# Layer 1 of a recommendation tower: all four full steps as split products, the half step earlier, and one block of ten passes

## The reference

```
x0 = prev = stack of 32 gathered rows                   # [B, 32, D]
for W in (filter_0, filter_1):
    z    = einsum('bhd,bmd->bhmd', x0, prev)            # all pairs of fields
    prev = relu(einsum('bpd,pn->bnd', z as [b, h*m, d], W[0]))   # [B, 128, D]
    outs.append(prev)
z = sum over d of concat(outs)                          # [B, 256]
h = relu([z, dense_ctx] @ W_top1 + b_top1); h = relu(h @ W_top2 + b_top2)
y = h @ W_top3                                          # [B, 1]
```

## Time and profile before

| what | value |
|---|---|
| median of 3 runs | 951.88 us (946.05 to 952.69) |
| the profiled execution's own time | 947.22 us, span 945.3 us |
| TensorE busy | 881.0 us (93%) |
| GpSimd busy | 773.2 us (82%) |
| VectorE busy | 765.0 us (81%) |
| ScalarE busy | 691.3 us (73%) |
| granted TensorE clock | 0.998 of full speed |
| DMA | 58.13 MB, mean 61 GB/s |

### The profile page before, as it was taken

The page is one execution under the profiler, slowest core; times in us unless marked ns, Lnnn a source line. Parts: engine busy times, 40 slices in busy tenths (PEclk is TensorE's granted clock), DMA queues, the critical chain, the costliest instruction groups (busy, mean ns, idle before and its releaser), DMA issues.

```text
span 945.3 us, 17955 instructions
## 1 busy us (share of the span) xinstructions
PE 881.0 (93%) x3551; PEld 650.2 (69%) x3551; DVE 765.0 (81%) x2391; ACT 691.3 (73%) x2347; POOL 773.2 (82%) x582
## 2 busy tenths in 40 slices
PE   0289999999999999999999999999999999999989
PEld 0157777777777777777777777777777777777753
DVE  4068888889888888898888889988888899888893
ACT  2058777787878777878787778787877777877762
POOL 7768899888888999988889989887777877777772
PEclk9999999999999999999999999999999999999999
DMA  6031222222112222221122222211222222102000
GB/s 175 13 105 51 75 75 75 73 72 71 32 50 70 73 74 73 74 71 34 46 69 74 73 74 74 74 38 37 67 71 71 71 71 71 47 29 66 1 1 0
DMA packets 41436, 58.13 MB, mean 61 GB/s; under 512 B 7265, under 2 KB 16033, under 8 KB 41410
## 3 DMA queue, kind: packets, MB, share of 16 engines
q1 hardware_dynamic: 37314, 55.76, 18.6%
q0 software_dynamic: 4096, 2.11, 1.4%
HBM read 54.79 MB, written 3.05 MB: 61 GB/s over the span
## 4 chain that ended last, share of the span: by engine, by line
PE 53%; DVE 26%; issue 14%; POOL 4%; DVEq 2%; DMA 0%; ACT 0%
PE bank L836 38%; DVE acc L721 18%; PE bank L774 12%; POOL rows L331 4%; DVE pair L587 4%; DVE cur_low L598 2%; DVE parts L721 1%; DVEq L718 1%; PE bank L879 1%; DVEq L240 0%; PE bank L866 0%; PE bank L867 0%; DVE sum L629 0%; PE bank L874 0%; DVEq L707 0%
## 5 line engine op out<-in xcount | busy, mean ns | idle before, releaser
L521 ACT ACTIVATE parts<-bank,x 128x128 f32<-128x128 f32 x2048 | 584.8, 385 | 143.5 <-PE bank L836 140.1
L721 DVE SCALAR_TENSOR_TENSOR acc<-bank,x,acc 128x128 f32<-128x128 f32 x1792 | 485.6, 343 | 97.2 <-PE bank L836 96.0
L836 PE MATMUL bank<-w_high,cur_high 128*128 128x512 f32 x1024 | 440.5, 430 | 10.9 <-DVE acc L721 10.0
L836 PE MATMUL bank<-w_low,cur_high 128*128 128x512 f32 x1024 | 401.4, 392 | 0.0
L836 PE MATMUL bank<-w_high,cur_low 128*128 128x512 f32 x992 | 389.1, 392 | 0.0
L352 POOL TENSOR_TENSOR half<-parts 128x1024 f32<-128x1024 f32 x127 | 307.1, 2418 | 92.4 <-DVE parts L721 91.9
L836 PEld LDWEIGHTS bank<-w_high,cur_high 128*128 128x128 f32 x1024 | 192.5, 188 | 105.9 <-DVE acc L721 29.3
L836 PEld LDWEIGHTS bank<-w_low,cur_high 128*128 128x128 f32 x1024 | 193.0, 188 | 48.8 <-issue 14.8
L836 PEld LDWEIGHTS bank<-w_high,cur_low 128*128 128x128 f32 x992 | 186.4, 188 | 41.8
L352 POOL TENSOR_TENSOR half<-half 128x512 f32<-128x512 f32 x127 | 165.5, 1303 | 10.0
L378 POOL DMA_INDIRECT rows_next<-table_dram,ids_next x96 | 92.5, 963 | 17.5 <-issue 7.0
(11 more groups left out here) (77 smaller groups left out, 485.8 us busy)
## 6 DMA issues: line engine op xcount, KB each, us to landing
shifts<-x_scratch SPq DMA_DIRECT2D x155, 256.0 KB
x<-x_scratch SPq DMA_DIRECT2D x31, 256.0 KB, 2.9
x_scratch<-turned SPq DMA_DIRECT2D x31, 64.0 KB, 1.5
rows_next<-table_dram,ids_next POOLq DMA_INDIRECT x96
wt<-w_top_dram SPq DMA_DIRECT2D x2, 512.0 KB, 8.9
x_scratch<-turned SPq DMA_DIRECT2D x31, 32.0 KB, 1.8
rows<-table_dram,ids_sb POOLq DMA_INDIRECT x32, 2.4
w_sb<-w_ab_dram SPq DMA_DIRECT2D x1, 256.0 KB
```

Source lines behind the costliest of these rows:

```text
L521: ins = nc.scalar.activation(parts[q][ab][:, at:at + N2], act_bank[ab][:, i * N2:(i + 1) * N2], ACT.Copy, scale=x0[u][:, h, 2 * q + ab:2 * ...
L721: nc.vector.scalar_tensor_tensor(out=dst, in0=dve_bank[e % 2 * 2 + ab][:, i * N2:(i + 1) * N2], scalar=x0[u][:, h, 2 * q + ab:2 * q + ab + ...
L836: return nc.tensor.matmul(dst[:], cur_half[u][:, cols], w1_half[:, fields], **flags)
```

## The change

Four groups of edits. (1) `SPLIT` takes all four full steps, so steps 3 and 4 too are three fast passes; ScalarE rounds two more high parts, GpSimd subtracts two more low parts. (2) Step 0 moves from VectorE's slot 8 to slot 4, step 3 from 4 to 8, low16 ahead of step 4's pair; the turn moves to ScalarE's slot 0, TensorE's tile 4, ScalarE's slot 5. (3) Steps 1, 2, 3 and 0 are multiplied in one block of ten passes after tile 20, step 4 after tile 23, in place of five places from 17 to 24. (4) GpSimd no longer makes the first, 1024-wide addition of a tile: it issues a DMA that adds one half of `parts` to the other (`add_halves`), after one 1-column instruction on `mark`, and waits for it before the two smaller additions. It adds the two halves of `left` itself (`sum_left`); ScalarE rectifies the total into PSUM at slot 20, and VectorE's addition at slot 24 goes, with the fold moved there from slot 28. The low parts of steps 1 and 2 stand in the second half's stretch of GpSimd's queue, those of 3 and 4 ahead of the first half's. The last tile of all is still summed on VectorE. Lines with declarations and the end are left out here.

```diff
-TREE = 3
-LEFTS = 2
+TREE = 2
+LAST_TREE = 3
...
-SPLIT = (1, 2)
-DVE_PAIR = {0: (1,), 4: (2, 3), 8: (0,), 12: (4,)}
+SPLIT = (1, 2, 3, 4)
+DVE_PAIR = {0: (1,), 4: (2, 0), 8: (3,), 12: (4,)}
 PAIR_ORDER = [step for steps in DVE_PAIR.values() for step in steps]
-ACT_PAIR_HIGH = {5: 1, 13: 2}
+ACT_PAIR_HIGH = {4: 1, 8: 2, 13: 3, 16: 4}
 ACT_HIGH16, DVE_LOW16 = 9, 12
-PE_PRODUCT = {17: 1, 19: 3, 21: 0, 23: 4, 24: 2}
-PRODUCT_ORDER = list(PE_PRODUCT.values())
+PE_PRODUCT = {20: (1, 2, 3, 0), 23: (4,)}
+PRODUCT_ORDER = [step for steps in PE_PRODUCT.values() for step in steps]
...
-ACT_TURN, PE_TURN, ACT_TURNED = 1, 6, 8
-ACT_LEFT, DVE_TOTAL, DVE_FOLD = 20, 24, 28
+ACT_TURN, PE_TURN, ACT_TURNED = 0, 4, 5
+ACT_TOTAL, DVE_FOLD = 20, 24
...
-        lefts = free[:, 0:LEFTS * DC * 2 * N2].rearrange("p (i t l n) -> p i t l n", i=LEFTS, t=DC, l=2)
-        left = [lefts[:, i, :, :, :] for i in range(LEFTS)]
+        left = free[:, 0:DC * 2 * N2].rearrange("p (t l n) -> p t l n", t=DC, l=2)
+        total = free[:, DC * 2 * N2:DC * 3 * N2]
...
+            def add_halves(pair_no, q, whole):
+                pool.wait_ge(act_prod, (pair_no + 1) * (2 * EACH))
+                pool.wait_ge(mac, (pair_no + 1) * (2 * MACS))
+                nc.gpsimd.tensor_tensor(mark[:], mark[:], mark[:], ALU.subtract)
+                width = EACH * HG * N2 // 2
+                for ab in range(2 if whole else 1):
+                    nc.gpsimd.dma_start(parts[q][ab][:, 0:width], parts[q][ab][:, width:2 * width],
+                                        accum_op=ALU.add).then_inc(added[ab], 16)
             def sum_parts(chunk, pair_no, t):
                 tile = pair_no * 2 + t % 2
-                src, width, at = parts[t // 2 % 2][t % 2], EACH * HG * N2 // 2, 0
-                if t % 2 == 0:
-                    pool.wait_ge(act_prod, (pair_no + 1) * (2 * EACH))
-                    pool.wait_ge(mac, (pair_no + 1) * (2 * MACS))
-                for level in range(TREE):
-                    if level > 0:
-                        pool.wait_ge(tree, tile * TREE + level)
-                    if level == TREE - 1:
-                        dst = left[t // DC % LEFTS][:, t % DC, :, :].rearrange("p l n -> p (l n)")
-                        if t % DC == 0:
-                            pool.wait_ge(left_free, chunk + 1)
-                    else:
-                        dst = half[:, at:at + width]
-                    nc.gpsimd.tensor_tensor(dst, src[:, 0:width], src[:, width:2 * width],
-                                            ALU.add).then_inc(tree, 1)
-                    src, at, width = dst, at + width, width // 2
+                pool.wait_ge(added[t % 2], (pair_no + 1) * 16)
+                src = parts[t // 2 % 2][t % 2]
+                nc.gpsimd.tensor_tensor(half[t % 2][:], src[:, 0:512], src[:, 512:1024], ALU.add).then_inc(tree, 1)
+                pool.wait_ge(tree, tile * TREE + 1)
+                nc.gpsimd.tensor_tensor(left[:, t % DC, :, :].rearrange("p l n -> p (l n)"),
+                                        half[t % 2][:, 0:256], half[t % 2][:, 256:512], ALU.add).then_inc(tree, 1)
+            def sum_left(chunk):
+                pool.wait_ge(tree, (chunk + 1) * (DC * TREE))
+                pool.wait_ge(total_rectified, chunk + 1)
+                nc.gpsimd.tensor_tensor(total.rearrange("p (t n) -> p t n", t=DC), left[:, :, 0, :], left[:, :, 1, :],
+                                        ALU.add).then_inc(totalled, 1)
             def pair_lows(c, which):
@@ -359,8 +369,7 @@
                     step = SPLIT[i]
                     pool.wait_ge(pair_high_done, (c - 1) * len(SPLIT) + i + 1)
-                    pool.wait_ge(multiplied, products_before(c, step))
-                    nc.gpsimd.tensor_tensor(pair_low[step][:], pair[step - 1][:], pair_high[step][:].bitcast(FP32),
+                    nc.gpsimd.tensor_tensor(pair_low[step - 1][:], pair[step - 1], pair_high[step][:].bitcast(FP32),
                                             ALU.subtract).then_inc(pair_low_done, 1)
...
             def block_body(k, next_block, one_after):
-                for t in range(tiles if next_block else tiles - 1):
-                    if t % DC == DC - 1 and (next_block or t < tiles - DC - 1):
-                        pair_lows(k * CPB + t // DC + 2, (0,))
+                for t in range(0, tiles, 2):
+                    whole = next_block or t < tiles - 2
                     if t % DC == 0 and (next_block or t < tiles - DC):
-                        pair_lows(k * CPB + t // DC + 1, range(1, len(SPLIT)))
-                    sum_parts(k * CPB + t // DC, k * (tiles // 2) + t // 2, t)
-                    if next_block and t == rows_at:
-                        pool.wait_ge(gathered, (k + 1) * (F * 16))
-                        nc.gpsimd.tensor_copy(
-                            rows[:, bass.ds(k + 1, 1), :, :].rearrange("p o f d -> p (o f d)"),
-                            rows_next[:].rearrange("p f d -> p (f d)")).then_inc(rows_ready, 1)
-                        if one_after:
-                            fetch_ids(k + 2)
-                            pool.wait_ge(rows_ready, k + 2)
-                    if (next_block and t < rows_at) or (one_after and t > rows_at):
-                        for f in late[t]:
-                            gather(f)
+                        pair_lows(k * CPB + t // DC + 1, (2, 3))
+                    add_halves(k * (tiles // 2) + t // 2, t // 2 % 2, whole)
+                    for s in (t, t + 1):
+                        if (next_block and s < rows_at) or (one_after and s > rows_at):
+                            for f in late[s]:
+                                gather(f)
+                    if t % DC == 2 and (next_block or t < tiles - DC - 2):
+                        pair_lows(k * CPB + t // DC + 2, (0, 1))
+                    for s in (t, t + 1) if whole else (t,):
+                        sum_parts(k * CPB + t // DC, k * (tiles // 2) + t // 2, s)
+                        if s % DC == DC - 1:
+                            sum_left(k * CPB + t // DC)
+                        if next_block and s == rows_at:
+                            pool.wait_ge(gathered, (k + 1) * (F * 16))
+                            nc.gpsimd.tensor_copy(
+                                rows[:, bass.ds(k + 1, 1), :, :].rearrange("p o f d -> p (o f d)"),
+                                rows_next[:].rearrange("p f d -> p (f d)")).then_inc(rows_ready, 1)
+                            if one_after:
+                                fetch_ids(k + 2)
+                                pool.wait_ge(rows_ready, k + 2)
...
-        def act_left(act, c, u, pairs_before):
-            act.wait_ge(tree, (c + 1) * (DC * TREE))
+        def act_total(act, c, pairs_before):
+            act.wait_ge(totalled, c + 1)
             act.wait_ge(paired, pairs_before)
-            nc.scalar.copy(x4_bank[:].rearrange("p (t n) -> p t n", t=DC),
-                           left[u][:, :, 0, :]).then_inc(left_copied, 1)
+            nc.scalar.activation(x4_bank[:], total, ACT.Relu).then_inc(total_rectified, 1)
         def act_pair_high(act, c, step):
             act.wait_ge(paired, paired_at(c, step))
-            wait(act, multiplied, products_before(c, step))
-            nc.scalar.copy(pair_high[step][:], pair[step - 1][:]).then_inc(pair_high_done, 1)
+            nc.scalar.copy(pair_high[step][:], pair[step - 1]).then_inc(pair_high_done, 1)
...
-                if step in SPLIT:
-                    wait(dve, pair_low_done, (c - 2) * len(SPLIT) + SPLIT.index(step) + 1)
...
-        def dve_total(dve, c, u):
-            dve.wait_ge(left_copied, c + 1)
-            half_total = x4_bank[:].rearrange("p (t n) -> p t n", t=DC)
-            nc.vector.tensor_tensor(half_total, half_total, left[u][:, :, 1, :], ALU.add).then_inc(left_free, 1)
-        def dve_fold(dve, c, k, total):
-            dve.wait_ge(left_free, c + LEFTS + 1)
-            s2 = sum2[:, bass.ds(k, 1), :, :].rearrange("p o t n -> p (o t n)")
-            nc.vector.scalar_tensor_tensor(
-                out=s2, in0=total, scalar=0.0, in1=s2, op0=ALU.max, op1=ALU.add).then_inc(folded, 1)
+        def block_sum(k):
+            return sum2[:, bass.ds(k, 1), :, :].rearrange("p o t n -> p (o t n)")
+        def dve_fold(dve, c, k):
+            dve.wait_ge(total_rectified, c + 2)
+            nc.vector.tensor_tensor(block_sum(k), x4_bank[:], block_sum(k), ALU.add).then_inc(folded, 1)
...
-                            if slot == DVE_TOTAL and not (first and u == 0):
-                                dve_total(dve, c - 1, 1 - u)
                             if not (last and u == UNROLL - 1):
+                                if slot == DVE_LOW16:
+                                    dve_low16(dve, c + 1)
                                 for step in DVE_PAIR.get(slot, ()):
                                     dve_pair(dve, c + 1, 1 - u, step, turn=not last)
```

(24 more changed lines are left out.)

46 lines of the change are left out of this document (26 added, 20 removed).

## The result

| | before | after |
|---|---|---|
| median of the runs made together (4 and 4) | 948.96 us (945.13 to 952.69) | 922.49 us (921.67 to 923.40) |
| ratio, 95% interval | | 0.972 (0.967 to 0.977) |
| the profiled execution's own time, span | 947.22, 945.3 us | 921.67, 919.8 us |

The change makes the kernel 2.8% faster. The spread of the kernel before is the clock's: in the experiments' sets its executions with a mean granted clock of 0.998 or more take 945.5 to 947.8 us, those with 0.993 take 951.9 to 953.0. Between the profiled executions the change is worth 25.6 us; forecast were 31.7. First, from the page after: busy times, the chain by engine, the first small addition, the adding DMA (KB each, us to landing).

What follows compares the result with a forecast made beforehand. TensorE and VectorE took turns setting the 26.80 us period; afterwards GpSimd would set 25.85 with gathers, those two 25.35 without. 947.22 minus 31.7 is 915.5; with the median 4.66 above that execution, forecast 919 us, range 895 to 985.

Steps and rivals of the forecast that it cites:

- Leg A: The part of a chunk's period where TensorE works without a break, tile 13 to 27: from 15.07 to 14.05 us.
- leg B: The rest of the period, VectorE behind until TensorE may write a VectorE bank again: from 11.73 to 11.3 us.
- The split's 0.32: TensorE's first-layer products: splitting two plain float32 steps (0.86 to 0.70 us each) saves 0.32 us a chunk.
- the fold's 0.6: VectorE's fold into `sum2`, moved from slot 28 to idle time at slot 24: 0.6 us off the path.
- The 0.3 for ScalarE's lateness: TensorE's gap at tile 16: step 0 in slot 4 ends ScalarE's 1.09 us wait, saving 0.3 us a chunk.
- GpSimd's loop: GpSimd's queue of 25.0 us plus 0.85 of DMA waits sets the period in chunks with gathers: 25.85 us.
- The sum: 30 periods, 20 with gathers at 25.85 and 10 at 25.35, save 33.5 us; the end costs 1.8: 31.7 less.
- The end: VectorE waits for GpSimd's last tile, now with an adding DMA: 7.7 us for 5.93, so 1.8 more.
- The two reads of an adding transfer: GpSimd's adding DMA reads two sources, so runs at half a copy's rate: landing 4.9 us; 4.1 was taken.
- the second rival: GpSimd becomes the bound, waiting for the first half's DMAs; landing 4.9 us gives 972 us; chance 0.25.
- TensorE waiting for GpSimd's low part inside the block: In the ten-pass block after tile 20; listed as a sign that the prediction is wrong, no size given.
- VectorE idle for `turned`: In VectorE's slot 4, behind step 2's pair; listed as a sign of being wrong; 0.05 us put down, 1.0 at most.

Runs made afterwards that it cites:

- late low parts: The changed kernel with step 3 multiplied after tile 22 and step 4 after tile 24, out of the block after tile 20: 909.1 us, ratio 0.960.

## Why the prediction was right, and where its reason was not

The forecast was 919 with a range of 895 to 985; 922.49 came. Its sign and size are right, its mechanism half.

**Leg A and leg B** hold. Without gathers leg A is 672.51 to 686.63, 14.12 us (forecast 14.05); its end is taken, as in the earlier trace rows, 0.27 behind the start of VectorE's group at 686.36. Leg B, to the next tile 13 at 698.23, is 11.60, and 11.45 in the chunk before (forecast 11.3): the fold gives its 0.6 back, `turned` takes up to 0.17 in every second chunk, and in every other one VectorE takes 0.27 longer around the sum of `acc`, as it did before in every second. The period is 25.57 to 25.78 instead of 25.35. The split's 0.32 and the fold's 0.6 are shown alone, 0.33 and 0.43. The 0.3 for ScalarE's lateness is the one that was mis-sized, as far as shown: with the low parts late, undoing it costs 0.05, but only half of ScalarE's wait comes back with it.

**GpSimd's loop** was forecast at 25.85, and 25.87 came, for another reason. Step by step: an adding DMA's issue takes 0.93 (1.25 assumed); a gather behind another DMA has a pitch of 1.37 (1.25); the landing is 3.7 us after the issue's end (4.1); the waits are 0.82 (0.85). So GpSimd's own round, without its idle time at `mark`, is 25.89 - 0.95 = 24.9, not 25.85, and it does not bind. What binds is one stretch of its queue, from the second half's `mark` to step 3's low part; where GpSimd stands 0.24 to 0.27 longer in it, the period is 0.36 longer. The prediction named that low part as where GpSimd's lateness would pass on, "for which TensorE stands in the block 1.4 us after its start", but priced it only as the end of the whole loop; it should have priced the stretch as a leg of its own. That the two came to the same number is chance, and late low parts shows it: the waits stay and 13.4 us go.

**The sum** was 31.7 us and 25.6 came between the profiled executions. Too much was forecast by 10.8 for the 20 periods with gathers (26.39 for 25.85; the two stalled periods hold 4.8 + 3.5 of it, of which the fall of the clock is about 1.6 in the second, the five longer periods 1.9) and by 2.8 for the 10 periods without gathers (25.63 for 25.35). Too little by 2.8 for the 30 periods before (26.89 on average, not 26.80), by 3.2 for the last chunk, which has no layer 1 in it and which I left out (24.4 us from its `cur_low` to the first product for 27.6), and by 1.6 for the start. The end came as forecast, 1.87 for 1.8. The median then came nearer than the sum, and that is luck: I had added 4.66 for the distance of the median, which for the kernel before is a matter of the clock, and the execution after lies 0.82 below its own median. (915.5 + 4.66 would be 920.2; the 919 is 1.2 below its own sum.)

**The rivals.** The two reads of an adding transfer are borne out by the landings, and yet the second rival stayed away: 3.7 us is below the 4.6 at which the DMA waits would have reached the old period, and an issue was 0.32 cheaper than assumed. Of the signs named, "TensorE waiting for GpSimd's low part inside the block" was among the wrong ones, and it came; so was VectorE idle for `turned`, which came with 0.17.

**Open.** Why the last chunk is 3.2 us shorter was not tried; with the large additions back on GpSimd it takes 26.4 us, with half the data added 23.4, so GpSimd's sums are part of it. Nor is it shown what GpSimd does in its two stalls, or in the 0.24 to 0.27 before some of its DMAs; shown is that the first stall goes when the loop goes, and that the second gets shorter with the bytes added.

## What to carry to other kernels

When an engine serves several consumers in one queue, price each stretch from what starts it to the first instruction that someone waits for, not only the whole round; idle time right behind a wait says that the wait costs nothing. A block of products needs the inputs of its later products soon after its start: moving two products one and two tiles back was worth half as much as the whole change.

## What the hardware showed that was not expected

- Issuing an adding DMA of 512 KB takes GpSimd 0.93 us, a copying one of the same shape 0.57 (each half of a pair).
- A long loop on GpSimd stands 3.25 us where it jumps back. Written out, it has no such stall but 0.26 us before the DMAs of each second half. A stall of 1.90 us before a gather is there with and without the loop, and 0.61 with half the bytes in the adding DMAs.
- Behind a wait of 2.27 us TensorE's granted clock fell to 0.50 in one execution, behind one of 2.29 at the same place it stayed at 1.00 in another; the periods are 29.39 and 27.83.
- At the end of late low parts the granted clock falls to 0.50, TensorE's level of 1.2 GHz, after 8.4 us of products that alternate between 128 and 16 rows. The changed kernel makes the same products and keeps 1.00, and so does late low parts with step 0 back in slot 8. Ten passes that take it 2.57 us (1.65 + 0.92) take 4.50 at the lower clock. Busy time by stretch of late low parts (the us of each engine, then the clock, DMA share and GB/s):

```profile
884.00:886.00 2.00, 2.00 (x5) 0.59 (x4) 0.00 (x0) 0.00 (x0) 0.36 (x1) 1.00 0.53 98
...
888.00:890.00 2.00, 1.34 (x4) 0.52 (x2) 1.90 (x4) 0.00 (x0) 0.00 (x0) 0.50 0.00 0
...
894.00:896.00 2.00, 2.00 (x6) 0.95 (x5) 0.00 (x0) 1.72 (x3) 0.00 (x0) 1.00 0.02 4
```
